# Folding a normalisation's mean into the weights of the first product of a ViT block

## The chip, the cores and the metric

One Trainium2 chip, one core of it. The metric is device time in microseconds of one execution, median over runs. All inputs lie in HBM before the kernel starts and the output is written back to HBM.

## The reference, cut to what matters

64 images of 3x96x96 are cut into 6x6 patches of 16x16x3 = 768 pixels. With `layernorm(x) = (x - mean) / sqrt(var + 1e-5)`:

```python
x = layernorm(x) * ln1_g + ln1_b             # over 768 pixels
x = x @ W + bias                             # 768 -> 256
x = layernorm(x) * ln2_g + ln2_b + pe        # over 256
h = concat(cls_token + cls_pos, x)           # 37 tokens an image
h = h + attention(layernorm(h))              # 16 heads of 16, rotary positions
h = h + ffn(layernorm(h))                    # 256 -> 1024 -> 256, ternary weights, 8-bit tokens
```

## The kernel before, in words

The 2368 tokens (class tokens included, as rows of zeros in x) lie in 19 tiles of 128 rows, `t` = 0 to 18, the last with 64 rows. The program has three stages: the patch stage (from pixels to rotated q and k and to values), attention over 32 pairs of images, and the feed-forward stage. The change is in the patch stage.

Each engine runs a list of instructions in the order in which it is written; semaphores (`S[...]`) tie the lists together. On each engine the patch stage is a loop over steps `s`, and `patch_step(s)` works on several tiles at once: the pixels of tile s or s + 1, the product's result of tile s - 2, the second normalisation of tile s - 3, and q, k and v of tile s - 9 and later (LAG is 9). So q, k and v begin at step 9; TensorE runs `early_step(s)` before that and `patch_step(s)` from then on. In one step:

- VectorE (DVE) takes statistics of the pixels (`pixel_stats`, L661, `pixel_mean`, L668, `pixel_var`, L674), statistics of the product's result (`y_stats`, L680, `y_mean`, L685, `y_var`, L690), centres and scales that result by ln2_g (`y_centre`, L695), makes h (`h_first`, L703) and takes its statistics (L709, L715, L720). From step 10 on it also rotates q and k (L775, L783).
- GpSimd (POOL) turns each variance into 1/sqrt (`inverse_root`, L1158), makes -mean/sd (`shift`, L1171), adds the two halves of the rotation (L1165) and writes the one-hot rows `hot` (L1187).
- ScalarE (ACT) normalises the pixels of a tile (`pixels_normal`, L979), copies the transposed pixels out of PSUM (`pixels_out`, L986), and does the same two things for h (L992, L999).
- TensorE (PE) turns the normalised pixels (six transposes, `turn_pixels`, L390), multiplies them by W (six f32 matmuls of 128x256, `patch_product`, L400), adds an offset row with a bf16 matmul on one-hot rows (`product_offset`, L383), puts the position rows into PSUM (`position_rows`, L383 too), turns h (`turn_h`, L430), and makes q, k and v (L443, L421). A f32 matmul stands as two in the profile.

Before the loop DVE multiplies W by ln1_g (L739, six instructions), TensorE makes the row ln1_b @ W (`patch_offset`, L369), and DVE and ACT split the offset and position rows into three bf16 parts that add up to f32 (L728, L1044, L1046). The SP queue loads the pixels and weights: x(0), the two halves of W, x(1), x(2), then the rest, where x(4) to x(7) each wait for a tile that ACT has normalised (`x_norm`). Five small loads go out on ACT's queue.

## Time and profile before

| | us |
|---|---|
| median of 3 runs | 355.41 (354.68 to 358.23) |
| the profiled execution, its own time | 358.58 |
| its span in the profile | 356.8 |
| PE busy | 310.9 (87%) |
| DVE busy | 247.1 (69%) |
| ACT busy | 214.6 (60%) |
| POOL busy | 136.8 (38%) |

A share of busy time is a mean over three stages with different limits, so the stages are read apart. In the span the patch stage reaches to about 175 us, attention to about 262 us, and the feed-forward stage to the end. The granted clock is TensorE's, as a share of its full speed.

### The profile page before, as it was taken

What the parts mean: (1) busy time and instruction counts of PE and PEld (TensorE: products, weight loads), DVE (VectorE), ACT (ScalarE), POOL (GpSimd) and SP (SyncE); (2) the same over time, 40 slices, a digit from 0 to 9 for tenths busy, and PEclk for the clock granted to TensorE, in tenths of its full rate; (3) what the DMA queues carried; (4) which work ended last, traced back from release to release, by engine and by line L of the source; (5) the groups of instructions that cost most, each with busy time, mean ns of one, the idle gap of its engine ahead of it and who ended that gap; (6) DMA issues with size and microseconds to landing.
All of it is one profiled execution on the core that took longest, in us unless ns stands there. A gap on an engine that the chain in (4) does not pass through costs nothing.

```text
span 356.8 us, 9434 instructions
## 1 busy us (share of the span) xinstructions
PE 310.9 (87%) x3582; PEld 235.8 (66%) x3590; DVE 247.1 (69%) x647; ACT 214.6 (60%) x385; POOL 136.8 (38%) x262
## 2 busy tenths in 40 slices
PE   7385767999999999799799999999976899999884
PEld 6274656777777765465488778778754677776553
DVE  2616647677566736245558787788758999999982
ACT  2224445447576453344556665665635999999992
POOL 1215453556545524444392000000035566555630
PEclk9878999999999999899989999999999999999998
DMA  7952991000000000001311121221100001000011
GB/s 230 264 187 88 376 322 33 3 17 33 16 16 32 17 18 17 31 31 49 72 38 40 42 50 39 45 45 40 25 3 1 2 24 38 29 31 29 30 46 51
DMA packets 19291, 22.30 MB, mean 63 GB/s; under 512 B 2304, under 2 KB 15888, under 8 KB 19248
## 3 DMA queue, kind: packets, MB, share of 16 engines
q1 hardware_dynamic: 18544, 20.89, 19.5%
q10 hardware_dynamic: 704, 0.82, 0.9%
q8 instruction: 29, 0.48, 0.6%
q14 instruction: 14, 0.11, 0.1%
HBM read 16.68 MB, written 5.02 MB: 61 GB/s over the span
## 4 chain that ended last, share of the span: by engine, by line
PE 62%; DVE 19%; ACT 8%; issue 5%; DMA 3%; POOL 2%; SPq 0%; DVEq 0%; ACTq 0%
PE ps L400 14%; PE ps L443 10%; PE ps L524 9%; PE ps L547 7%; DVE sc L900 7%; PE ps L421 4%; DVE ximg L921 4%; PE ps L514 4%; PE ps L390 3%; DMA ximg<-in_x 3%; PE ps L532 3%; ACT ximg L1124 3%; PE ps L383 2%; PE ps L451 2%; ACT ximg L1119 2%
## 5 line engine op out<-in xcount | busy, mean ns | idle before, releaser
L1158 POOL TENSOR_TENSOR rs<-rs,nhalf 128x1 f32<-128x1 f32 (+1 forms) x76 | 41.7, 556 | 181.4 <-DVE rs L894 100.5
L400 PE MATMUL ps<-w_in,xT 128*128 128x256 f32 (+1 forms) x228 | 56.6, 401 | 5.8 <-ACT xT L986 5.8
L400 PEld LDWEIGHTS ps<-w_in,xT 128*128 128x128 f32 (+1 forms) x228 | 43.9, 200 | 12.9 <-ACT xT L986 6.3
L1076 ACT ACTIVATE ximg<-ps 128x296 f32<-128x296 f32 x64 | 26.6, 418 | 31.4 <-PE ps L524 30.8
L443 PE MATMUL ps<-w_qk,hnT 128*128 128x512 f32 (+1 forms) x76 | 37.3, 615 | 2.3 <-DVE h L703 2.3
L775 DVE TENSOR_TENSOR qa<-ps,tab 128x512 f32<-128x512 f32 (+1 forms) x19 | 13.1, 691 | 36.9 <-PE ps L383 36.9
L838 DVE TENSOR_REDUCE ximg<-ps 128x16 f32<-128x592 f32 x32 | 24.7, 773 | 16.5 <-PE ps L514 16.4
L524 PE MATMUL ps<-tab,ximg 128*128 128x128 f32 x256 | 35.7, 283 | 0.0
L1165 POOL TENSOR_TENSOR qa<-qa,qb 128x512 f32<-128x512 f32 (+1 forms) x19 | 24.1, 1267 | 15.6 <-DVE qb L783 15.6
L524 PEld LDWEIGHTS ps<-tab,ximg 128*128 128x128 f32 x256 | 28.1, 143 | 1.3
L986 ACT ACTIVATE xT<-ps 128x768 f32<-128x768 f32 (+1 forms) x19 | 15.0, 791 | 22.4 <-PE ps L390 18.6
L979 ACT ACTIVATE xn<-ximg,nmr,rs 128x768 f32<-128x768 f32 (+1 forms) x19 | 19.4, 1020 | 14.4 <-POOL nmr L1171 13.6
L547 PE MATMUL ps<-ximg 128*37 128x34 f32 x1024 | 25.7, 203 | 2.2 <-issue 1.7
L547 PEld LDWEIGHTS ps<-ximg 128*37 128x37 f32 x1024 | 22.3, 117 | 7.0 <-issue 2.7
L390 PE MATMUL ps<-tab,xn 128*128 128x128 f32 (+1 forms) x114 | 15.9, 277 | 11.4 <-ACT xn L979 11.4
L842 DVE TENSOR_TENSOR ximg<-ps,ximg 128x592 f32<-128x592 f32 x32 | 24.8, 776 | 1.1
L1124 ACT ACTIVATE ximg<-ximg,magic,sc 128x1024 f32<-128x1024 f32 (+1 forms) x19 | 23.6, 1241 | 2.4 <-DVE sc L912 1.8
L921 DVE SCALAR_TENSOR_TENSOR ximg<-ps,sc,wide 128x1024 f32<-128x1024 f32 (+1 forms) x19 | 24.4, 1282 | 0.7 <-PE ps L606 0.7
L615 PE MATMUL ps<-tab,ximg 128*128 128x128 f32 (+1 forms) x152 | 20.0, 275 | 5.2 <-ACT ximg L1124 5.2
L900 DVE TENSOR_REDUCE sc<-ximg 128x1 f32<-128x1024 f32 (+1 forms) x19 | 23.0, 1209 | 2.1 <-ACT ximg L1119 1.8
L606 PE MATMUL ps<-w1t,ximg 128*128 128x512 bf16 (+1 forms) x68 | 18.1, 381 | 7.2 <-ACT ximg L1113 6.8
L999 ACT ACTIVATE hnT<-ps 128x256 f32<-128x256 f32 (+1 forms) x19 | 7.1, 373 | 26.8 <-PE ps L430 26.8
(107 smaller groups left out, 673.8 us busy)
## 6 DMA issues: line engine op xcount, KB each, us to landing
ximg<-in_x SPq DMA_DIRECT2D x18, 384.0 KB, 8.0
ximg<-vsc SPq DMA_DIRECT2D x64, 51.0 KB, 2.0
vsc<-vt SPq DMA_DIRECT2D x18, 136.0 KB, 1.7
out<-ximg SPq DMA_DIRECT2D x18, 128.0 KB, 1.7
ximg<-in_W SPq DMA_DIRECT2D x2, 1024.0 KB, 10.5
qkT<-in_W SPq DMA_DIRECT2D x2, 384.0 KB, 6.2
wide<-in_rows SPq DMA_DIRECT2D x1, 640.0 KB, 5.5
w_qk<-in_Wqk SPq DMA_DIRECT2D x1, 512.0 KB, 8.6
```

What stands on the lines that cost most here:

```text
L390: mm = pe.transpose(ps_xT[:, k, 0:n], xn[t % 2][0:n, 128 * k:128 * k + 128], ident[0:n, 0:n])
L400: pe.matmul(dst[0:n, :], xT[t % 2][:, k, 0:n], w_in[:, k, :], start=(k == 0), stop=False)
L443: pe.matmul(dst[0:n, :], hnT[t % HB][:, k, 0:n], w_qk[:, k, :], start=(k == 0), stop=False)
L524: mm = pe.transpose(ps[:, b, 128 * g:128 * g + 128], flat[:, at0:at0 + 128], ident)
L547: mm = pe.matmul(dst.rearrange("p (e c) -> p e c", e=2), pT[p % 2][:, g, i, :], rhs, start=True, stop=True)
L838: v.tensor_reduce(mx[u][:, :].rearrange("p (r h) -> p r h", r=4), ps_s, AX.X, ALU.max).then_inc(S["s_max"], 1)
L842: v.tensor_tensor(pr[u][:, :, 0:TOK].rearrange("p (r h) t -> p r h t", r=4), ps_s, mx[u][:, :].rearrange("p (r h) -> p r h", r=4).unsqueeze(3)
L900: v.tensor_reduce(sc[t % 8][0:n, c:c + 1], src[0:n, :], AX.X, ALU.max, apply_absolute_value=True).then_inc(S[f"{x}_amax"], 1)
L921: v.scalar_tensor_tensor(out=hd[t % 3][0:n, :], in0=ps_f[0:n, :], scalar=sc[t % 8][0:n, 3:4], in1=fb1[0:n, :], op0=ALU.mult, op1=ALU.add). ...
L1076: act.activation(pT[p % 2][:, g0:g0 + 4, :, :], ps_pT(b), ACT.Copy).then_inc(S[f"p_evac{b}"], 1)
L1124: act.activation(hd[t % 3][0:n, :], hd[t % 3][0:n, :], ACT.Identity, bias=magic[0:n, :], scale=sc[t % 8][0:n, 6:7]).then_inc(S["f_rnd"], 1)
L1158: pool.tensor_tensor(rs[u][0:n, i:i + 1], rs[u][0:n, i:i + 1], nhalf[0:n, :], ALU.pow).then_inc(S[done], 1)
```

## The change

The mean of a row of pixels is taken off through the weights. With W' = ln1_g * W and the mean over the 768 rows of W' taken off each of its columns, x @ W' no longer depends on the row's mean; the row's 1/sd is multiplied in behind the product, together with the offset row ln1_b @ W + bias.

- TensorE makes the column means before the loop (`weight_means`, six f32 matmuls with `g1s` = ln1_g / 768 as stationary operand), and DVE takes them off as it scales W (`w_in`, six instructions that read the mean row from PSUM, each with a semaphore increment of its own).
- ACT's `pixels_normal` is gone, and POOL's `shift` for pixels with it. TensorE turns the raw pixels as soon as they are loaded.
- DVE's new `y_scale` multiplies the product by 1/sd and adds `yoff`, from PSUM into the SBUF tile `ymid`; `y_stats` and `y_centre` read `ymid` instead of PSUM. It frees the product's PSUM bank, which `y_centre` did before.
- The offset's matmul on one-hot rows behind each product is gone. A class token's row is zeroed by POOL's new `leave_class`, which multiplies 1/sd of the second normalisation by a column of 0 and 1.
- DVE takes the pixel statistics of tile s - 1 in step s, where it took those of tile s + 1.
- The early steps of TensorE run the product of s - 1 ahead of the transposes of s; `patch_step` keeps its order but for the offset.
- On the SP queue the halves of W go out ahead of x(0), and no load of x waits for `x_norm`. The small offset and table loads grow by 64 KB and 10 KB.

```diff
+        g1s = sb("g1s", [128, KP])
+        yoff = sb("yoff", [128, D])
...
-            load_x(0)
             sp.dma_start(w_raw[:, 0:3, :], w_rows[:, 0:3, :]).then_inc(S["ld_w0"], 16)
             sp.dma_start(w_raw[:, 3:6, :], w_rows[:, 3:6, :]).then_inc(S["ld_w1"], 16)
+            load_x(0)
             load_x(1)
+            sp.wait_ge(S["ld_offs"], 16)
             load_x(2)
-            sp.wait_ge(S["ld_offs"], 16)
             load_x(3)
+            sp.dma_start(w_o[:], a["Wo"].rearrange("(k p) n -> p k n", p=128)).then_inc(S["ld_o"], 16)
             sp.dma_start(offs[0:112, 4 * D:7 * D], spread_row(a["offsets"][4 * D:7 * D], 3 * D, 112)).then_inc(S["ld_rows"], 16)
-            sp.dma_start(w_o[:], a["Wo"].rearrange("(k p) n -> p k n", p=128)).then_inc(S["ld_o"], 16)
-            sp.wait_ge(S["x_norm"], 1)
             load_x(4)
+            load_x(5)
             sp.dma_start(w_qk[:], a["Wqk"].rearrange("(k p) n -> p k n", p=128)).then_inc(S["ld_qk"], 16)
-            sp.wait_ge(S["x_norm"], 2)
-            load_x(5)
+            load_x(6)
             sp.dma_start(w_v[:], a["Wv"].rearrange("(k p) n -> p k n", p=128)).then_inc(S["ld_v"], 16)
-            sp.wait_ge(S["x_norm"], 3)
-            load_x(6)
+            load_x(7)
             sp.dma_start(tab[:, FTAB:NTAB], a["table"][:, FTAB:NTAB]).then_inc(S["ld_rot"], 16)
-            sp.wait_ge(S["x_norm"], 4)
-            load_x(7)
+            load_x(8)
             sp.dma_start(wide[:, D:2 * D + F], spread_row(a["rows"][D:2 * D + F], D + F)).then_inc(S["ld_wide"], 16)
-            for t in range(8, NT + 1):
+            for t in range(9, NT + 1):
...
+            def weight_means():
+
+                pe.wait_ge(S["g1_done"], 1)
+                for k in range(KP):
+                    if k % 3 == 0:
+                        pe.wait_ge(S[f"ld_w{k // 3}"], 16)
+                    mm = pe.matmul(ps_mean, bass.AP(g1s, k, [[KP, 128], [0, 128]]), w_raw[:, k, :],
+                                   start=(k == 0), stop=(k == KP - 1))
+                mm.then_inc(S["mrow"], 1)
+
             def patch_offset():
-                pe.wait_ge(S["ld_w0"], 16)
-                pe.wait_ge(S["ld_byp"], 16)
                 for k in range(KP):
-                    if k == 3:
-                        pe.wait_ge(S["ld_w1"], 16)
-                    mm = pe.matmul(ps[0:K3, 6, 0:D], bass.AP(byp, k, [[2 * KP + 2, 128], [0, K3]]), w_raw[:, k, :],
+                    mm = pe.matmul(ps_off, bass.AP(byp, k, [[2 * KP + 2, 128], [0, 128]]), w_raw[:, k, :],
                                    start=(k == 0), stop=(k == KP - 1))
                 mm.then_inc(S["crow"], 1)
...
             def turn_pixels(t):
-                pe.wait_ge(S["x_norm"], t + 1)
+                pe.wait_ge(ld_x[t], 16)
+                if t == 0:
+                    pe.wait_ge(S["ld_tab"], 16)
                 war(pe, "x_evac", t, 1)
                 n = rows(t)
                 for k in range(KP):
-                    mm = pe.transpose(ps_xT[:, k, 0:n], xn[t % 2][0:n, 128 * k:128 * k + 128], ident[0:n, 0:n])
+                    mm = pe.transpose(ps_xT[:, k, 0:n], ximg[0:n, t, 128 * k:128 * k + 128], ident[0:n, 0:n])
                 mm.then_inc(S["x_turned"], 1)
 
             def patch_product(t):
                 pe.wait_ge(S["x_evac"], t + 1)
-                war(pe, "y_mid", t)
-                if t == 0:
-                    pe.wait_ge(S["wg_done"], 2)
+                war(pe, "y_scaled", t)
+                if t == 16:
+                    pe.wait_ge(S["w_rc"], 1)
                 n, dst = rows(t), ps_y(t % 2)
                 for k in range(KP):
-                    pe.matmul(dst[0:n, :], xT[t % 2][:, k, 0:n], w_in[:, k, :], start=(k == 0), stop=False)
-                if t >= 2:
-                    product_offset(t)
-
-            def product_offset(t):
-
-                if t >= 2:
-                    pe.wait_ge(S["hot_done"], min(t, 16))
-                add_rows(ps_y(t % 2)[0:rows(t), :], t, C_ROWS).then_inc(S["y_ready"], 1)
+                    if t == 0:
+                        pe.wait_ge(S["wg_done"], k + 1)
+                    mm = pe.matmul(dst[0:n, :], xT[t % 2][:, k, 0:n], w_in[:, k, :], start=(k == 0),
+                                   stop=(k == KP - 1))
+                mm.then_inc(S["y_ready"], 1)
 
             def position_rows(t):
+                if t == 0:
+                    pe.wait_ge(S["b_done"], 1)
+                pe.wait_ge(S["hot_done"], max(1, min(t, 16)))
                 war(pe, "h_ready", t, 1)
                 add_rows(ps_pos[0:rows(t), :], t, PE_ROWS, only=True).then_inc(S["pos_ready"], 1)
...
             def early_step(s):
+                patch_product(s - 1)
                 turn_pixels(s)
-                patch_product(s - 1)
                 if s == 5:
                     out_offset()
-                position_rows(s - 2)
-                turn_h(s - 3)
+                if live(s - 2, NT + 1):
+                    position_rows(s - 2)
+                if live(s - 3, NT + 1):
+                    turn_h(s - 3)
...
+            weight_means()
+            turn_pixels(0)
             patch_offset()
-            pe.wait_ge(S["ld_tab"], 16)
-            turn_pixels(0)
-            patch_product(0)
-            turn_pixels(1)
-            patch_product(1)
-            turn_pixels(2)
-            pe.wait_ge(S["hot_done"], 1)
-            pe.wait_ge(S["b_done"], 1)
-            product_offset(0)
-            product_offset(1)
-            position_rows(0)
-            for s in range(3, LAG):
+            for s in range(1, LAG):
...
+            def y_scale(t):
+                v.wait_ge(S["y_ready"], t + 1)
+                v.wait_ge(S["x_rstd"], t + 1)
+                if t == 0:
+                    v.wait_ge(S["y_off"], 1)
+                n = rows(t)
+                v.scalar_tensor_tensor(out=ymid[t % 2][0:n, :], in0=ps_y(t % 2)[0:n, :], scalar=rs[t % 2][0:n, 0:1],
+                                       in1=yoff[0:n, :], op0=ALU.mult, op1=ALU.add).then_inc(S["y_scaled"], 1)
+
             def y_stats(t):
-                v.wait_ge(S["y_ready"], t + 1)
-                n = rows(t)
-                v.bn_stats(st[t % 2][0:n, 2, :], ps_y(t % 2)[0:n, :]).then_inc(S["y_stat"], 1)
+                v.wait_ge(S["y_scaled"], t + 1)
+                n = rows(t)
+                v.bn_stats(st[t % 2][0:n, 2, :], ymid[t % 2][0:n, :]).then_inc(S["y_stat"], 1)
...
-                v.scalar_tensor_tensor(out=ymid[t % 2][0:n, :], in0=ps_y(t % 2)[0:n, :], scalar=mv[t % 2][0:n, 1, 0:1],
+                v.scalar_tensor_tensor(out=ymid[t % 2][0:n, :], in0=ymid[t % 2][0:n, :], scalar=mv[t % 2][0:n, 1, 0:1],
...
+            v.wait_ge(S["ld_byp"], 16)
+            v.tensor_scalar(g1s[:, :], g1, 1.0 / PD, None, ALU.mult).then_inc(S["g1_done"], 1)
             pixel_stats(0)
             pixel_mean(0)
             pixel_var(0)
-            v.wait_ge(S["ld_byp"], 16)
-            for half in range(2):
-                v.wait_ge(S[f"ld_w{half}"], 16)
-                for k in range(3 * half, 3 * half + 3):
-                    ins = v.tensor_scalar(w_in[:, k, :], w_raw[:, k, :], g1[:, k:k + 1], None, ALU.mult)
-                ins.then_inc(S["wg_done"], 1)
+            v.wait_ge(S["mrow"], 1)
+            for k in range(KP):
+                v.scalar_tensor_tensor(out=w_in[:, k, :], in0=w_raw[:, k, :], scalar=g1[:, k:k + 1], in1=ps_mean,
+                                       op0=ALU.mult, op1=ALU.subtract).then_inc(S["wg_done"], 1)
             pixel_stats(1)
             pixel_mean(1)
             pixel_var(1)
+            v.wait_ge(S["ld_offs"], 16)
+            v.wait_ge(S["crow"], 1)
+            v.tensor_tensor(yoff[:, :], ps_off, bfix, ALU.add).then_inc(S["y_off"], 1)
             v.wait_ge(S["ld_tab"], 16)
-            v.wait_ge(S["ld_offs"], 16)
             v.tensor_tensor(cls0, cls0, cls1, ALU.add).then_inc(S["bmix"], 1)
             v.wait_ge(S["ld_pe"], 16)
...
+            y_scale(0)
+            y_stats(0)
             v.wait_ge(S["b_hi"], 1)
             leave_out(bres[0:K3, py], bhi[0:K3, py], 0, brow[0:K3, :]).then_inc(S["b_res"], 1)
+            y_mean(0)
+            y_var(0)
...
-                if live(s - 2, NT + 1):
-                    y_stats(s - 2)
+                if live(s - 2, NT + 1) and s > 2:
+                    y_scale(s - 2)
                 if s == 16:
                     weight_scales()
-                if live(s + 1, NT + 1):
-                    pixel_stats(s + 1)
-                if live(s - 2, NT + 1):
+                if live(s - 1, NT + 1) and s > 2:
+                    pixel_stats(s - 1)
+                if live(s - 2, NT + 1) and s > 2:
+                    y_stats(s - 2)
+                if live(s - 1, NT + 1) and s > 2:
+                    pixel_mean(s - 1)
+                if live(s - 2, NT + 1) and s > 2:
                     y_mean(s - 2)
-                if live(s + 1, NT + 1):
-                    pixel_mean(s + 1)
-                if live(s - 2, NT + 1):
                     y_var(s - 2)
-                if live(s + 1, NT + 1):
-                    pixel_var(s + 1)
+                if live(s - 1, NT + 1) and s > 2:
+                    pixel_var(s - 1)
...
-            def pixels_normal(t):
-                act.wait_ge(ld_x[t], 16)
-                act.wait_ge(S["x_nmr"], t + 1)
-                war(act, "x_turned", t)
-                n = rows(t)
-                act.activation(xn[t % 2][0:n, :], ximg[0:n, t, :], ACT.Identity, bias=nmr[t % 2][0:n, 0:1],
-                               scale=rs[t % 2][0:n, 0:1]).then_inc(S["x_norm"], 1)
...
+            def leave_class(t):
+
+                pool.wait_ge(S["y_root"], t + 1)
+                n = rows(t)
+                pool.tensor_tensor(rs[t % 2][0:n, 1:2], rs[t % 2][0:n, 1:2], tab[0:n, tile_o + t:tile_o + t + 1],
+                                   ALU.mult).then_inc(S["y_rstd"], 1)
...
-                    inverse_root(1, s - 2, s % 2, "y_var", "y_rstd")
-                if live(s + 1, NT + 1):
-                    inverse_root(0, s + 1, (s + 1) % 2, "x_var", "x_rstd")
-                    shift(0, 0, s + 1, "x_rstd", "x_nmr")
+                    inverse_root(1, s - 2, s % 2, "y_var", "y_root")
+                    leave_class(s - 2)
+                if live(s - 1, NT + 1) and s > 2:
+                    inverse_root(0, s - 1, (s - 1) % 2, "x_var", "x_rstd")
```

The start of TensorE's list before (`onesf` is the warm-up's operand, `tab` holds the identity, `xn` the normalised pixels, `xT` the turned ones, `hot` and `pos_rows` the one-hot and offset rows):

```order
L486 MATMUL ps<-onesf 128x128 x13
L369 MATMUL ps<-qkT,byp 111x256 x6
L390 MATMUL ps<-tab,xn 128x128 x6
L400 MATMUL ps<-w_in,xT 128x256 x6
L390 MATMUL ps<-tab,xn 128x128 x6
L400 MATMUL ps<-w_in,xT 128x256 x6
L390 MATMUL ps<-tab,xn 128x128 x6
L383 MATMUL ps<-pos_rows,hot 128x256 x3
```

And now, up to the first position rows (`ximg` holds raw pixels, W lies in `qkT` at this time):

```order
L499 MATMUL ps<-onesf 128x128 x13
L373 MATMUL ps<-qkT,g1s 128x256 x6
L402 MATMUL ps<-tab,ximg 128x128 x6
L379 MATMUL ps<-qkT,byp 128x256 x6
L414 MATMUL ps<-w_in,xT 128x256 x6
L402 MATMUL ps<-tab,ximg 128x128 x6
L414 MATMUL ps<-w_in,xT 128x256 x6
L402 MATMUL ps<-tab,ximg 128x128 x6
L393 MATMUL ps<-pos_rows,hot 128x256
```

The means of W come first, the transposes read the raw pixels, and the first two offset matmuls are gone.

DVE's list in an early step before, from the statistics of one product to the h made of it:

```order
L680 BN_STATS st<-ps 128x6
L661 BN_STATS st<-ximg 128x6 x2
L685 BN_AGGR mv<-st 128x2
L668 BN_AGGR mv<-st 128x2
L690 TENSOR_SCALAR rs<-mv 128x1
L674 TENSOR_SCALAR rs<-mv 128x1
L695 SCALAR_TENSOR_TENSOR ymid<-ps,mv,wide 128x256
L703 SCALAR_TENSOR_TENSOR h<-ymid,rs,ps 128x256
```

And now:

```order
L685 SCALAR_TENSOR_TENSOR ymid<-ps,rs,yoff 128x256
L665 BN_STATS st<-ximg 128x6 x2
L691 BN_STATS st<-ymid 128x6
L671 BN_AGGR mv<-st 128x2
L696 BN_AGGR mv<-st 128x2
L701 TENSOR_SCALAR rs<-mv 128x1
L676 TENSOR_SCALAR rs<-mv 128x1
L706 SCALAR_TENSOR_TENSOR ymid<-ymid,mv,wide 128x256
L714 SCALAR_TENSOR_TENSOR h<-ymid,rs,ps 128x256
```

One instruction more (L685), the statistics of the result behind those of the pixels, and L706 with both of its tensors in SBUF.

## Rows read from the trace of the kernel before

**Rows 1.** Stretch, length, busy us of PE, PEld, DVE, ACT, POOL; granted clock, DMA, GB/s

```profile
10.00:20.00 10.00, 5.01 (x19) 3.96 (x20) 6.97 (x18) 3.76 (x5) 3.75 (x6) 0.77 0.97 287
40.00:50.00 10.00, 6.31 (x35) 4.79 (x33) 6.43 (x25) 4.33 (x7) 5.51 (x15) 1.00 1.04 342
100.00:120.00 20.00, 20.00 (x103) 15.20 (x102) 12.74 (x43) 12.29 (x25) 10.66 (x20) 1.00 0.06 22
```

**Rows 2.** Waits from 0 to 66 us: total us, times, longest

```profile
DVE h L703 <- PE ps L383: 13.5, 4, 4.5
```

**Rows 3.** Timeline (start, us, engine, line, [idle before]): the start, all engines

```profile
3.89 1.02 DVE L661 BATCH_NORM_STATS2 st<-ximg 128x6 f32<-128x384 f32 x2 [2.88 <-DMA ximg<-in_x]
...
10.06 0.88 DVE L739 TENSOR_SCALAR w_in<-qkT,byp 128x256 f32<-128x256 f32 x3 [3.85 <-DMA qkT<-in_W]
...
17.20 5.33 PE L400 MATMUL ps<-w_in,xT 128*128 128x256 f32 x12 [4.92 <-ACT xT L986]
...
23.21 0.81 ACT L986 ACTIVATE xT<-ps 128x768 f32<-128x768 f32 x1 [3.19 <-PE ps L390]
24.07 2.46 PEld L400 LDWEIGHTS ps<-w_in,xT 128*128 128x128 f32 x12 [1.14 <-ACT xT L986]
...
30.12 0.48 DVE L703 SCALAR_TENSOR_TENSOR h<-ymid,rs,ps 128x256 f32<-128x256 f32 x1
```

**Rows 4.** Timeline: one unhindered turn of DVE's loop, with POOL beside it

```profile
57.61 1.00 DVE L661 BATCH_NORM_STATS2 st<-ximg 128x6 f32<-128x384 f32 x2
...
58.53 0.17 DVE L685 BATCH_NORM_AGGREGATE mv<-st 128x2 f32<-128x6 f32 x1
...
58.78 0.11 DVE L690 TENSOR_SCALAR rs<-mv 128x1 f32<-128x1 f32 x1
...
58.97 0.47 DVE L695 SCALAR_TENSOR_TENSOR ymid<-ps,mv,wide 128x256 f32<-128x256 f32 x1
58.97 1.06 POOL L1158 TENSOR_TENSOR rs<-rs,nhalf 128x1 f32<-128x1 f32 x2 [0.60 <-DVE rs L690]
...
59.55 0.48 DVE L703 SCALAR_TENSOR_TENSOR h<-ymid,rs,ps 128x256 f32<-128x256 f32 x1
...
60.07 0.43 DVE L709 BATCH_NORM_STATS2 st<-h 128x6 f32<-128x256 f32 x1
...
60.82 0.42 DVE L680 BATCH_NORM_STATS2 st<-ps 128x6 f32<-128x256 f32 x1
```

**Rows 5.** Timeline: PE at the first instruction of step 9, and DVE behind it

```profile
65.92 0.28 PE L383 MATMUL ps<-pos_rows,hot 111*128 111x256 bf16 x1 [0.46 <-DVE h L703]
...
66.25 1.00 DVE L728 SCALAR_TENSOR_TENSOR pos_rows<-qkT,tab 111x768 bf16<-111x768 bf16 x1
```

**Rows 6.** Timeline: POOL's shift beside a DVE instruction with two SBUF inputs

```profile
14.71 0.48 DVE L751 SCALAR_TENSOR_TENSOR qkT<-qkT,tab 111x256 f32<-111x256 f32 x1
14.79 0.53 POOL L1171 TENSOR_SCALAR nmr<-mv,rs 128x1 f32<-128x1 f32 x1
```

**Rows 7.** The line of that shift: duration ns min/median/max over the kernel

```profile
L1171 POOL TENSOR_SCALAR nmr<-mv,rs x38: 257/265/550, 6.3 to 149.7; 128x1 f32<-128x1 f32 x36, 64x1 f32<-64x1 f32 x2
```

**Rows 8.** Timeline: PE through a step of the later patch stage

```profile
99.77 0.27 PE L383 MATMUL ps<-pos_rows,hot 111*128 111x256 bf16 x1
...
100.32 2.76 PE L400 MATMUL ps<-w_in,xT 128*128 128x256 f32 x12
102.92 0.28 PE L383 MATMUL ps<-pos_rows,hot 111*128 111x256 bf16 x1
103.03 0.82 PE L390 MATMUL ps<-tab,xn 128*128 128x128 f32 x6
...
106.71 0.27 PE L383 MATMUL ps<-pos_rows,hot 111*128 111x256 bf16 x1
```

**Rows 9.** Timeline: the stall at the end of the products

```profile
143.94 0.47 DVE L703 SCALAR_TENSOR_TENSOR h<-ymid,rs,ps 64x256 f32<-64x256 f32 x1 [1.04 <-POOL rs L1158]
...
144.56 3.22 PE L443 MATMUL ps<-w_qk,hnT 128*128 128x512 f32 x4 [2.26 <-DVE h L703]
```

More of the change, by code:

```diff
@@ L73, in shape_constants @@
             pe[r] = np.concatenate([np.sin(ax), np.cos(ax), np.sin(ay), np.cos(ay)])
-    return np.concatenate([np.eye(128), vmask, pmask, taken, patch, ~patch, hot, pe,
+    return np.concatenate([np.eye(128), vmask, pmask, taken, patch, ~patch, hot, by_tile, pe,
                            cos.reshape(128, -1), sin.reshape(128, -1)], 1).astype(np.float32)
-FTAB = 128 + NH + 2 + 2 + 2 + TOK + D
+FTAB = 128 + NH + 2 + 2 + 2 + TOK + NT + 1 + D
 NTAB = FTAB + 2 * (NT + 1) * HD
@@ L212, in two @@
             return [sb(f"{name}{u}", shape, dt) for u in range(2)]
-        xn = two("xn", [128, PD])
         xT = two("xT", [128, KP, 128])
@@ L729, in leave_out @@
                                               op0=ALU.mult, op1=ALU.add)
-            qo, py = slice(2 * D, 5 * D), slice(0, 2 * D)
+            qo, py = slice(D, 4 * D), slice(0, D)
+            v.wait_ge(S["ld_byp"], 16)
+            v.tensor_scalar(g1s[:, :], g1, 1.0 / PD, None, ALU.mult).then_inc(S["g1_done"], 1)
             pixel_stats(0)
@@ L1037, in patch_step @@
                     pixels_out(s)
-            pixels_normal(0)
-            pixels_normal(1)
             pixels_out(0)
-            qo, py = slice(2 * D, 5 * D), slice(0, 2 * D)
-            act.wait_ge(S["bmix"], 5)
+            pixels_out(1)
+            qo, py = slice(D, 4 * D), slice(0, D)
+            act.wait_ge(S["bmix"], 3)
             act.activation(bhi[0:K3, py], brow[0:K3, :], ACT.Copy).then_inc(S["b_hi"], 1)
@@ L1046, in _ @@
             act.activation(bmid[0:K3, py], bres[0:K3, py], ACT.Copy).then_inc(S["b_mid"], 1)
-            pixels_normal(2)
-            pixels_out(1)
             pixels_out(2)
@@ L1205, in _ @@
                 patch_step(s)
-            pool.wait_ge(S["x_norm"], NT)
+            pool.wait_ge(S["y_scaled"], NT)
+            for u in range(2):
+                ins = pool.memset(pr[u][:, :, TOK:64], 0.0)
+            ins.then_inc(S["p_zero"], 1)
             for u in range(4):
@@ L1210, in _ @@
                 patch_step(NT + 3 + u)
-            for u in range(2):
-                ins = pool.memset(pr[u][:, :, TOK:64], 0.0)
-            ins.then_inc(S["p_zero"], 1)
             for s in range(NT + 7, NT + LAG + 2):
```

45 lines of the change are left out of this document (18 added, 27 removed).

## The prediction

> **What bounds the kernel now.** I read the stretches of the span first, then the waits of the first 66 us, then the timeline of three places: the start, the early steps, and one late step. Late in the patch stage TensorE is never idle: 20.00 us busy of 20, at a granted clock of 1.00 [rows 1]. A step takes 106.71 - 99.77 = 6.94 us there [rows 8], all of it TensorE's. [...] In the first 66 us DVE waits 13.5 us, in four waits, for the position rows that TensorE writes late [rows 2], because its transposes wait for ACT's normalised pixels, and these for 1/sd from POOL. At the start TensorE is idle 4.92 us ahead of its first product and runs that at the lower clock, 5.33 us for twelve records against 2.76 later [rows 3, 8]. The first h is made at 30.12 us and step 9 begins at 65.92 [rows 3, 5], so the six turns of the early loop between them took 5.9 us each, where an unhindered turn of DVE takes 3.5 (60.82 - 57.61, and 0.33 for the first statistics [rows 4]). What is saved ahead of 65.92 moves all that follows; work taken off ACT in the late steps moves nothing.
>
> **The start, walked with the new lists.** The third transfer of SP's queue (the second half of W) let DVE go at 10.06, and the first (x(0)) had landed at 3.89 [rows 3]. Now x(0) is the third, with 74 KB more on the other queue, which at the 287 GB/s of the stretch from 10 us on [rows 1] is 0.3 us: x(0) at 10.4, both halves of W long before. The column means are a product's six matmuls, 102.92 - 100.32 = 2.6 us [rows 8], from the end of the warm-up at 6.0, so they are done at 8.6, under the wait for x(0). The statistics of x(0) come ahead of the scaling of W on DVE and take 1.45 us, to 11.85. The six scalings now read PSUM and the mean row, and I cost them like h's STT at 59.55, 0.50 each by start to start [rows 4], where plain ones took 0.29 [rows 3]: W' complete at 14.85, 3.0 us against 1.8. TensorE meanwhile turns x(0), 0.65 us (0.82 less the overlap [rows 8]), makes the offset row to 13.7, and runs the first product, which follows the slices of W', to 16.3. The second one waits for its transposes (16.9), ACT's copy and 0.86 us from the copy's start to the product's [rows 3], and ends at 20.6; the third transposes at 21.25, then the position rows of tile 0. DVE does the statistics of x(1) to 16.3, four row instructions of 0.48 to 18.2, `y_scale` and `y_stats` to 19.2, and the three-way split with ACT, at half the width of before, in some 1.6 to 20.8, so both sides meet and the first h is made at **21.6**, 8.5 us earlier. Lower bound: DVE alone, 21.3. [...]
>
> **The early steps.** Two loops could set them. TensorE's: transposes 0.82 to their end, then ACT's copy to the product 0.86, then the product 2.60 [rows 3, 8], together 4.3 us; the product now stands ahead of the next transposes, so ACT's copy is no longer hidden there. DVE's, from `y_scale` round to the next: `y_scale` 0.45 (between the 0.35 of an offset-free stats start and the 0.52 of h's), pixel statistics 58.53 - 57.61 = 0.92, `y_stats` 0.42, the first aggregate 0.15, the second aggregate to POOL's root 58.97 - 58.53 = 0.44, root to h (below), h to its statistics 0.52, and those to the next step 60.82 - 60.07 = 0.75 [rows 4]. Root to h was 59.55 - 58.97 = 0.58. It gets `leave_class` in between, which no row shows. Its ends are POOL's shift, 0.27 [rows 7], and its root, the same kind of instruction on the same size with a power, 0.53 of a pair in 1.06 [rows 4]; I take 0.27, because it multiplies as the shift does, plus 0.10 to issue. And `y_centre` now reads two SBUF tensors, starting when POOL's root starts (both at 58.97 [rows 4]). Such a pair stands at 14.7: a shift beside a DVE instruction with two SBUF inputs took 0.53 and ended 0.13 behind it, where the median is 0.265 and only a few rows reach 0.55 [rows 6, 7]. So POOL's reads waited. The root then ends about 0.33 later (DVE's 0.47, plus the root's own 0.41 behind its reads, less the usual 0.55). Root to h: 0.58 + 0.37 + 0.33 = 1.28. The loop is 0.45 + 0.92 + 0.42 + 0.15 + 0.44 + 1.28 + 0.52 + 0.75 = **4.93 us**, so DVE with POOL sets the pace, not TensorE. Bounds of the turn: 4.6 without the collision, 5.2 with `leave_class` at 0.53.
>
> [...]
>
> Six turns are 29.6 us; two inserted instructions (the add at step 5, 0.5, and the 768-wide split at step 6, 1.0 as its like [rows 5]) were there before too. From 21.6 this gives h of tile 6 at 52.7 and step 9 at 53.2 instead of 65.92: **-12.7 us**. The loads keep up: up to x(8) they are 6.8 MB, 24 us at the 287 GB/s of the second slice [rows 1], and x(8) is turned at about 48.
>
> **The late steps.** The offset matmul goes, 103.03 - 102.92 = 0.11 us of TensorE [rows 8], in the eleven tiles from 8 to 18: **-1.2 us**. DVE was busy 12.74 of 20 us [rows 1], 4.4 us a step; what the early turn gains, 4.93 - 3.54 = 1.4, makes it 5.8, still inside 6.83, so TensorE stays full. ACT's 1.03 us less a tile is worth nothing here. At the end of the products TensorE stood 2.26 us for the last h, which waited for POOL's root, and this costs it the clock too [rows 9]; `leave_class` adds 0.4 to that wait: **+0.4 us**. POOL clears the attention's buffers in another order, behind which nobody waits by 161 us. Attention and feed-forward do not change.
>
> **Sum.** -12.7 - 1.2 + 0.4 = -13.5 us. On the profiled execution, 358.58, that is 345.1; it stands 3.2 us above the median of the three runs, 355.41, and the change is at places all runs share, so I forecast the median **342.0 us**.
>
> **Rivals.**
> (a) The pace of the early steps does not fall. If some other hand-over (`h_normal` ahead of `pixels_out` on ACT, TensorE in order behind `turn_h`) keeps a turn at 5.9, only the start is won: 355.4 - 8.5 - 1.2 + 0.4 = 346.3. For it: the old loop also had 3.5 us of DVE work and took 5.9. Against: the waits that made it so hang on the normalised pixels, which are gone. 0.16.
> (b) No collision and short hand-overs, a turn of 4.6: 2.0 us better, 340.0; with a little less at the start, 338.5. 0.17.
> (c) TensorE loses its clock. In the early steps it will work 3.6 of 4.9 us. [...] For it: after gaps of 4.9 and 2.26 us the clock was low [rows 3, 9]. Against: from 40 to 50 us TensorE was busy 6.3 of 10 us and had 1.00 [rows 1]. Slower 0.03, about even 0.03.
> [...]
> (d) DVE's late step outgrows 6.83. [...] It is the lesser brother of (a) and I give it 0.06.
> The forecast's own case has 0.55.
>
> **Range and chances.** The forecast's case spans 339.5 to 345 by the bounds of the turn (6 x 0.3 either way) and 1 us of landing time. (b) reaches to 338, (a) and (d) to 346.5, and the runs of one kernel here differ by 3.5 us. 337.5 to 347.5 leaves out (c) and the tails, under 2 in 10. A measurement of this kernel can tell about 1%, 3.6 us, from no change: faster 0.94, same 0.03, slower 0.03.
>
> **What would show it.** TensorE's first product near 13.7 us at the full clock; the first h at 21 to 22; h of the early tiles 4.9 us apart, with POOL's root beside `y_centre` at 0.8 to 0.9 instead of 0.55; the first q and k product near 57 instead of 69; later steps 6.83 us apart and TensorE without idle time; the stall at the last tile 2.7 us long. It is wrong if DVE waits for TensorE in the early steps, if the granted clock of 10 to 50 us stays below 0.9, or if the late steps grow.

## The result, and the profile after

The changed kernel takes 341.55 us (median of 4 runs, 340.69 to 343.08), the kernel before 355.22 in the same series (354.68 to 358.23): a ratio of 0.9605, 95% interval 0.9549 to 0.966. The forecast was 342.0, with 337.5 to 347.5 as its range. The profiled execution took 343.08 against 358.58, its span 341.3 against 356.8; the text below accounts for these 15.5 us.

Busy times of the whole span, after:

```profile
PE 310.8 (91%) x3583; PEld 235.1 (69%) x3583; DVE 254.7 (75%) x666; ACT 197.1 (58%) x366; POOL 139.6 (41%) x262
```

ACT lost 17.5 us of work (197.1 against 214.6), DVE gained 7.6, TensorE is as busy as before. So what was saved is TensorE's waiting. The stretches, with the columns of [rows 1]:

```profile
10.00:20.00 10.00, 9.10 (x48) 7.83 (x47) 8.04 (x22) 2.34 (x4) 4.26 (x7) 1.00 0.96 324
...
40.00:50.00 10.00, 7.36 (x40) 5.67 (x38) 8.33 (x28) 3.87 (x7) 5.79 (x13) 1.00 0.62 211
50.00:60.00 10.00, 9.64 (x37) 7.21 (x38) 7.61 (x23) 2.50 (x5) 4.93 (x11) 0.83 0.01 2
...
100.00:120.00 20.00, 20.00 (x100) 14.89 (x99) 14.43 (x47) 8.45 (x20) 10.17 (x18) 1.00 0.06 22
```

From 10 to 20 us TensorE went from 5.01 busy at a clock of 0.77 to 9.10 at 1.00. The one bad row is new: from 50 to 60 us the clock is 0.83. The kernel before had low rows early, too, 0.77, 0.89 and 0.83 from 10 to 40 us. In the first of its six turns:

```profile
32.12 1.26 PE L390 MATMUL ps<-tab,xn 128*128 128x128 f32 x6 [4.21 <-ACT xn L979]
33.17 4.10 PE L400 MATMUL ps<-w_in,xT 128*128 128x256 f32 x12
```

These two took 1.8 us more than the 0.82 and 2.75 of the full clock, and the first product (5.33) took 2.6 more. So I estimate that some 4.4 us of the gain up to step 9 are clock that the kernel before had lost behind its waits; no run separates them from the shorter chain. DVE's waits for h in the first 53 us (step 9 begins at 50), as in [rows 2], which go to 66 us:

```profile
DVE h L714 <- POOL rs L1169: 3.6, 5, 0.7
DVE h L714 <- PE ps L393: 2.7, 2, 1.6
```

DVE's 13.5 us of waiting for the position rows has shrunk to 2.7, and five waits of 0.7 us for `leave_class` (L1169) on POOL have come in. One of the two waits for position rows is the first h, the other the third turn, where TensorE has the added work of step 5:

```profile
35.00 0.48 DVE L714 SCALAR_TENSOR_TENSOR h<-ymid,rs,ps 128x256 f32<-128x256 f32 x1 [1.07 <-PE ps L393]
```

The start, against [rows 3]:

```profile
6.74 3.01 PE L373 MATMUL ps<-qkT,g1s 128*128 128x256 f32 x12
8.66 1.02 DVE L665 BATCH_NORM_STATS2 st<-ximg 128x6 f32<-128x384 f32 x2 [4.75 <-DMA ximg<-in_x]
...
10.03 2.43 DVE L750 SCALAR_TENSOR_TENSOR w_in<-qkT,byp,ps 128x256 f32<-128x256 f32 x6
10.24 2.76 PE L379 MATMUL ps<-qkT,byp 128*128 128x256 f32 x12
...
12.83 2.75 PE L414 MATMUL ps<-w_in,xT 128*128 128x256 f32 x12
...
20.90 0.48 DVE L714 SCALAR_TENSOR_TENSOR h<-ymid,rs,ps 128x256 f32<-128x256 f32 x1 [1.62 <-PE ps L393]
```

Means, transposes, offset row and first product now follow one another on TensorE with little between them, and the product runs at the full clock. One turn of the early loop, from one h to the next, DVE and POOL:

```profile
25.48 0.48 DVE L714 SCALAR_TENSOR_TENSOR h<-ymid,rs,ps 128x256 f32<-128x256 f32 x1 [0.71 <-POOL rs L1169]
...
26.75 0.48 DVE L685 SCALAR_TENSOR_TENSOR ymid<-ps,rs,yoff 128x256 f32<-128x256 f32 x1
...
27.15 1.01 DVE L665 BATCH_NORM_STATS2 st<-ximg 128x6 f32<-128x384 f32 x2
...
28.08 0.41 DVE L691 BATCH_NORM_STATS2 st<-ymid 128x6 f32<-128x256 f32 x1
...
28.87 0.48 DVE L706 SCALAR_TENSOR_TENSOR ymid<-ymid,mv,wide 128x256 f32<-128x256 f32 x1
28.98 0.78 POOL L1156 TENSOR_TENSOR rs<-rs,nhalf 128x1 f32<-128x1 f32 x1 [1.13 <-DVE rs L701]
...
29.83 0.19 POOL L1169 TENSOR_TENSOR rs<-rs,tab 128x1 f32<-128x1 f32 x1
29.97 0.55 POOL L1156 TENSOR_TENSOR rs<-rs,nhalf 128x1 f32<-128x1 f32 x1
30.06 0.48 DVE L714 SCALAR_TENSOR_TENSOR h<-ymid,rs,ps 128x256 f32<-128x256 f32 x1 [0.71 <-POOL rs L1169]
```

30.06 - 25.48 = 4.58 us. The root beside `y_centre` took 0.78, the root of the pixels that follows it 0.55. Last, TensorE at step 9, at step 10 and at the last tile, against [rows 5] and [rows 9]:

```profile
50.36 0.27 PE L393 MATMUL ps<-pos_rows,hot 111*128 111x256 bf16 x1 [1.71 <-DVE h L714]
50.62 4.49 PE L414 MATMUL ps<-w_in,xT 128*128 128x256 f32 x12
...
58.65 0.28 PE L393 MATMUL ps<-pos_rows,hot 111*128 111x256 bf16 x1
...
130.05 3.65 PE L454 MATMUL ps<-w_qk,hnT 128*128 128x512 f32 x4 [2.70 <-DVE h L714]
```

Ahead of step 9 stands a wait of 1.71 us. The step itself, from 50.36 to 58.65, takes 8.29 us, and its product 4.49 where 2.75 is usual. Before, step 10 began here:

```profile
72.48 0.27 PE L383 MATMUL ps<-pos_rows,hot 111*128 111x256 bf16 x1
```

Step 9 took 72.48 - 65.92 = 6.56 us.

Where the 15.5 us came from, from landmarks of both traces:

| stretch | before | after | difference | forecast |
|---|---|---|---|---|
| up to the first h | 30.12 | 20.90 | -9.2 | -8.5 |
| to the start of step 9 | 35.80 | 29.46 | -6.3 | -4.2 |
| step 9 | 6.56 | 8.29 | +1.7 | -0.1 |
| to the stall at the last tile | 69.82 | 68.70 | -1.1 | -1.1 |
| that stall | 2.26 | 2.70 | +0.4 | +0.4 |
| behind it | 212.2 | 211.2 | -1.0 | 0 |

The terms add up to -15.5. The last row is none of the change's: the final 36.8 us of the trace before had a granted clock of 0.95, the same work after (35.8 us) had 1.00, and at the scores of the first attention group (166.05 and 151.54) the kernels are 14.5 apart. Ten of the twelve traces of the changed kernel and its variants also had a low clock (0.70 to 0.90) from 330 to 340 us. The medians differ by 13.7.

### The profile page after: what moved, and what is told of

Read it like the earlier page. It is cut to its first block, busy times and chain, and to the rows that moved or that the text cites. A ratio compares the mean times of both kernels' runs of the same rounds, so it can differ in the third digit from the quotient of the medians.

```text
span 341.3 us, 9410 instructions
## 1 busy us (share of the span) xinstructions
PE 310.8 (91%) x3583; PEld 235.1 (69%) x3583; DVE 254.7 (75%) x666; ACT 197.1 (58%) x366; POOL 139.6 (41%) x262
## 4 chain that ended last, share of the span: by engine, by line
PE 65%; DVE 20%; ACT 7%; issue 4%; POOL 2%; DVEq 0%
PE ps L414 13%; PE ps L454 10%; PE ps L528 9%; PE ps L551 7%; DVE sc L911 7%; PE ps L432 5%; PE ps L518 4%; DVE ximg L932 4%; PE ps L402 3%; PE ps L536 3%; ACT ximg L1122 3%; PE ps L462 2%; ACT ximg L1117 2%; PE ps L393 2%; PE ps L499 2%
## 5 line engine op out<-in xcount | busy, mean ns | idle before, releaser
L1156 POOL TENSOR_TENSOR rs<-rs,nhalf 128x1 f32<-128x1 f32 (+1 forms) x76 | 46.2, 607 | 164.4 <-DVE rs L905 100.8
L414 PE MATMUL ps<-w_in,xT 128*128 128x256 f32 (+1 forms) x228 | 54.8, 391 | 3.6 <-ACT xT L989 3.6
L414 PEld LDWEIGHTS ps<-w_in,xT 128*128 128x128 f32 (+1 forms) x228 | 42.2, 191 | 11.3 <-ACT xT L989 5.1
L528 PE MATMUL ps<-tab,ximg 128*128 128x128 f32 x256 | 35.8, 284 | 0.0
L610 PE MATMUL ps<-w1t,ximg 128*128 128x512 bf16 (+1 forms) x76 | 19.7, 382 | 5.7 <-ACT ximg L1111 5.6
L665 DVE BATCH_NORM_STATS2 st<-ximg 128x6 f32<-128x384 f32 (+1 forms) x38 | 19.2, 546 | 4.7 <-DMA ximg<-in_x 4.7
L1079 ACT ACTIVATE ximg<-ximg 128x592 f32<-128x592 f32 x32 | 22.6, 706 | 0.0
```

Source lines behind the costliest of these rows:

```text
L414: mm = pe.matmul(dst[0:n, :], xT[t % 2][:, k, 0:n], w_in[:, k, :], start=(k == 0), stop=(k == KP - 1))
L528: mm = pe.transpose(ps[:, b, 128 * g:128 * g + 128], flat[:, at0:at0 + 128], ident)
L1156: pool.tensor_tensor(rs[u][0:n, i:i + 1], rs[u][0:n, i:i + 1], nhalf[0:n, :], ALU.pow).then_inc(S[done], 1)
```

## The experiments

Each ratio below is against runs of the kernel before on the same chip; the runs were made in four groups, each on a chip of its own, so medians of different groups are compared by their ratios. Where and when the clock fell shows only in a trace, and each kernel has one. Five questions were open: what the load order is worth, what sets the early turn, whether ACT's relief matters, whether DVE has room late, and why step 9 is slow.

**The changed kernel again**, beside the next three:

> The changed kernel once more, as the reference of this group. 341.5 us, a ratio of 0.961 to the kernel before; first h near 20.9 us, step 9 of TensorE near 50.4 us, its product at the lower clock (4.5 us for twelve records against 2.76).

343.61 us, 0.9595 (0.9555 to 0.9636): the result stands. First h 20.72, step 9 at 50.18, its product 4.51 us long.

**Only the SP queue of the change** (order of the loads, and no load of x waiting for `x_norm`), in the kernel before:

```diff
-            load_x(0)
...
+            load_x(0)
...
-            sp.wait_ge(S["x_norm"], 1)
...
-            for t in range(8, NT + 1):
+            for t in range(9, NT + 1):
```

> The kernel before with only the SP queue of the change: W ahead of x(0), and no load of x waiting for a normalised tile. My theory: the gain comes from the shorter chain of hand-overs, not from the loads, so this is within 1 us of the kernel before (355). Rival: the loads carry the start, and with them alone the first h comes 5 us or more earlier and the time falls to 350 or below.

357.6 us, 1.0002 (0.9966 to 1.0038): nothing, as expected. Its first h is made at 29.21 instead of 30.12, and that is given back in the turns.

**x(0) first**, in the changed kernel:

```diff
+            load_x(0)
             sp.dma_start(w_raw[:, 0:3, :], w_rows[:, 0:3, :])
             sp.dma_start(w_raw[:, 3:6, :], w_rows[:, 3:6, :])
-            load_x(0)
```

> The changed kernel with x(0) ahead of the two halves of W on the SP queue. My theory: the start hangs on the third transfer of that queue, whichever it is. With W's second half third, the means of W end at about 11.4 instead of 9.6 us, W' is complete near 14.0 instead of 12.5, and the first h comes 1.2 to 1.6 us later; in time +1.2 to +1.6 us against the changed kernel. Rival: the order of the first three loads is indifferent, since both sides wait for both: 0.

345.88 us, 0.9676 (0.9627 to 0.9724). TensorE in the middle of the means:

```profile
10.01 1.56 PE L373 MATMUL ps<-qkT,g1s 128*128 128x256 f32 x6 [2.02 <-DMA qkT<-in_W]
```

The first h comes at 22.73, 2.0 us later than in the unchanged copy beside it, and the median is 2.3 later. That is more than the 1.2 to 1.6 expected. So the queue's new order is worth nothing by itself, and losing the one part of it that puts W ahead of x(0) costs 2 us once the means have to be read from W. Here the same wait of 1.71 us stood at step 9, and the product behind it took 2.83 us: the clock did not fall there. It fell at the last tile, whose product took 3.75.

**The scaled product stays in PSUM**, which takes one SBUF input from `y_centre` (POOL's root takes 0.78 us beside it):

```diff
-                v.scalar_tensor_tensor(out=ymid[t % 2][0:n, :], in0=ps_y(t % 2)[0:n, :], ...
+                v.scalar_tensor_tensor(out=ps_y(t % 2)[0:n, :], in0=ps_y(t % 2)[0:n, :], ...
```

The statistics and `y_centre` read `ps_y`, and TensorE's next product waits for `y_mid` instead of `y_scaled`.

> The changed kernel, with y_scale writing back to the product's PSUM bank; y_stats and y_centre read that, so y_centre has one SBUF input again. [...]

Expected were a root of 0.55 us, root to h in 0.85 instead of 1.08, a turn of 4.41 and 1 us in the time; if the root stayed at 0.78, nothing. Measured: 339.88 us, 0.9501 (0.9457 to 0.9545). The first two turns are 4.41 us, the last 4.35. `y_centre`, the root and h:

```profile
23.85 0.47 DVE L706 SCALAR_TENSOR_TENSOR ymid<-ps,mv,wide 128x256 f32<-128x256 f32 x1
23.96 0.55 POOL L1156 TENSOR_TENSOR rs<-rs,nhalf 128x1 f32<-128x1 f32 x1 [1.13 <-DVE rs L701]
...
24.87 0.48 DVE L714 SCALAR_TENSOR_TENSOR h<-ymid,rs,ps 128x256 f32<-128x256 f32 x1 [0.54 <-POOL rs L1169]
```

Same instructions, same moment, one operand in another memory: the root takes 0.55 instead of 0.78, `y_centre` 0.47 both times. The collision is real, costs POOL 0.23, and never held DVE's `y_centre`. The last turn shows it in full (4.58 - 0.23); in the first two TensorE's loop ends at 4.41, and with the added work of step 5 the third is 5.28, against 4.95 in `act_copy` (below) on the same chip. So the six turns together are 28.15 us, against 28.82 there: 0.7 us, where 1 us was expected. The median moved by 3.4 us (0.0094 of 357.8). What goes with the rest is the clock: in this trace it fell neither at step 9 nor at the last tile. That this is the effect of the edit is not shown.

```profile
49.23 0.27 PE L393 MATMUL ps<-pos_rows,hot 111*128 111x256 bf16 x1 [1.49 <-DVE h L714]
49.36 2.83 PE L414 MATMUL ps<-w_in,xT 128*128 128x256 f32 x12
...
126.91 1.95 PE L454 MATMUL ps<-w_qk,hnT 128*128 128x512 f32 x4 [2.52 <-DVE h L714]
```

**ACT gets its work back**: the raw pixels are copied by ACT before TensorE turns them, in the early steps too.

```diff
+                act.activation(xn[t % 2][0:n, :], ximg[0:n, t, :], ACT.Copy).then_inc(S["x_norm"], 1)
...
-                    mm = pe.transpose(ps_xT[:, k, 0:n], ximg[0:n, t, ...
+                    mm = pe.transpose(ps_xT[:, k, 0:n], xn[t % 2][0:n, ...
```

> The changed kernel with a copy of the raw pixels by ACT (1.03 us a tile) put back between load and transposes; statistics and 1/sd stay behind the product. My theory: the gain came from taking DVE's statistics and POOL's 1/sd out of the way to the transposes, not from the work that ACT is spared; so the early turns stay at 4.6 us, the late steps at 6.81 us, and the time rises by less than 1 us. Rival: the hop over ACT itself was the price; then the early turns go back towards 5.5 us or more and the time rises by 5 us.

343.6 us, 0.9594 (0.9554 to 0.9635): the same as without the copy. Turns are 4.58, late steps 6.81, and the product of step 9 took 2.83 behind its wait of 1.71. So ACT's time as such is free. That the early steps before were held by the dependence of ACT's output on POOL's 1/sd is then argued from the waits of the kernel before, here from 0 to 160 us (total, times, longest):

```profile
ACT xn L979 <- POOL nmr L1171: 13.6, 6, 7.7
PE ps L390 <- ACT xn L979: 11.4, 4, 4.2
```

The change also moved DVE's pixel statistics and TensorE's order; no run took these apart from it.

**One more DVE instruction a step**, in one kernel in steps 3 to 8, in another in steps 11 to 19:

```diff
+                if 3 <= s <= 8:
+                    v.bn_stats(spare[:, :], yoff[:, :])
```

> The changed kernel with one more DVE instruction (statistics of a 256 wide SBUF row, 0.42 us, result unused) behind y_scale in steps 3 to 8. My theory: DVE and POOL set the pace of the early turns, so each turn grows by 0.35 to 0.42 us, from 4.58 to 4.95 or 5.0, step 9 begins 2.3 us later and the time rises by 2.3 us. Rival: TensorE with ACT's copy sets the pace (4.41 us a turn), and the addition is hidden in part or whole, under 1 us.

> The changed kernel with the same added DVE instruction in steps 11 to 19 instead. My theory: TensorE is full there (6.81 us a step) and DVE has 1.1 us to spare, so the steps stay at 6.81 us and the time does not move (0 to 0.5 us, the half for step 19). Rival: DVE's longer step is already at the limit, and nine steps cost 3 to 4 us.

Early, DVE's h of the tiles:

```profile
25.33 0.48 DVE L715 SCALAR_TENSOR_TENSOR h<-ymid,rs,ps 128x256 f32<-128x256 f32 x1 [0.71 <-POOL rs L1172]
30.24 0.48 DVE L715 SCALAR_TENSOR_TENSOR h<-ymid,rs,ps 128x256 f32<-128x256 f32 x1 [0.71 <-POOL rs L1172]
35.14 0.48 DVE L715 SCALAR_TENSOR_TENSOR h<-ymid,rs,ps 128x256 f32<-128x256 f32 x1 [0.71 <-POOL rs L1172]
```

A turn is 4.90 us, 0.32 more, and the six turns take 30.40 us instead of 28.83. Five of the six were lengthened, by about 0.32 us each, so DVE with POOL sets the pace in them. The third was not (4.90 against 4.94): there TensorE, with the added work of step 5, set it before. Step 9 began 1.6 us later than in `act_copy` (51.46 against 49.88), where 2.3 was expected. The time itself is inconclusive: 342.45 us, 0.9568 (0.9512 to 0.9624), and the 1.6 us did not show in it. The runs go from 340.43 to 346.14. The trace is that of the longest run, whose product of step 9 took 5.42 us. Late, TensorE through two steps:

```profile
85.00 0.27 PE L394 MATMUL ps<-pos_rows,hot 111*128 111x256 bf16 x1
...
91.82 0.27 PE L394 MATMUL ps<-pos_rows,hot 111*128 111x256 bf16 x1
```

And a stretch of it, with the columns of [rows 1]:

```profile
100.00:120.00 20.00, 20.00 (x101) 14.79 (x99) 15.41 (x50) 8.44 (x21) 10.06 (x18) 1.00 0.07 22
```

Steps stay at 6.82, TensorE is never idle although DVE is busy 15.41 of 20 us, and the time is 344.28 us, 0.9609 (0.9558 to 0.966), that of the changed kernel. DVE has room there for this 0.4 us a step.

**The product of step 9 goes first**, ahead of the position rows that wait for DVE:

```diff
             def patch_step(s):
+                if s == 9:
+                    patch_product(s - 1)
+                    turn_pixels(s)
                 if live(s - 2, NT + 1):
                     position_rows(s - 2)
...
-                if live(s - 1, NT + 1):
+                if s > 9 and live(s - 1, NT + 1):
```

> The changed kernel, with TensorE in step 9 running the product of tile 8 and the transposes of tile 9 ahead of the position rows of tile 7, for which it waits 1.7 us today. My theory: that idle time (2.1 us from the end of the work before) and the lower clock behind it (4.49 against 2.76 us) are both lost to one wait, so both come back: step 10 begins near 55.6 instead of 58.65 us and the time falls by 3 us, to a ratio near 0.952. Rival: DVE sets the pace over step 10 too, and only the clock's 1.7 us or less comes back; or the clock falls at another place of the early steps and nothing is won.

340.69 us, 0.952 (0.9475 to 0.9566).

```profile
48.43 2.86 PE L414 MATMUL ps<-w_in,xT 128*128 128x256 f32 x12 [0.26 <-ACT xT L992]
...
55.25 0.27 PE L393 MATMUL ps<-pos_rows,hot 111*128 111x256 bf16 x1 [0.18 <-DVE h L717]
```

The product starts in what was the wait, at the full clock, and step 10 begins at 55.25 instead of 58.33. Of these 3.1 us, 1.65 are the shorter product (4.51 - 2.86), the rest is the wait that it fills. The kernel as a whole is 2.9 us under the copy beside it (343.61), as expected; the two intervals overlap by 0.001. The trace is that of its fastest run (338.99), and its clock was kept at the last tile too (1.96), which the edit does not touch.

**Filling both waits** of TensorE with matmuls on ones, whose result nobody reads, first too many (12 and 18, below), then as many as fit (7 and 11):

```diff
+                if s == 9:
+                    keep_busy(ps[:, 7, 0:128], 12)
...
+                if s == 20:
+                    pe.wait_ge(S["y_scaled"], 18)
+                    keep_busy(ps[:, 3, 0:128], 18)
```

> The changed kernel with matmuls of no use where TensorE waits longest: twelve f32 ones of 128x128 on ones ahead of the position rows of step 9, where it stands 1.7 us, and eighteen ahead of the q and k product of step 20, where it stands 2.7 us. They write PSUM that nobody reads, and fit into the waits. [...]

> The filled waits once more, at the right size. In the first attempt a f32 matmul of 128x128 took 0.22 us, not the 0.11 that I had counted, so 12 and 18 of them outlasted the waits by 0.6 and 1.3 us. Now 7 (1.6 us in a wait of 1.7) and 11 (2.4 us in one of 2.7). [...]

That the idle time is what lowers the clock was my supposition. With it I expected up to 3.5 us of the first (4.49 - 2.76 at step 9, 3.65 - 1.9 at the last tile) and 339.7 us, 0.950, of the second; if the clock fell all the same, no gain.

Too many: 341.47 us, 0.9556 (0.9507 to 0.9604); the fills lasted 2.84 and 4.18 us and overran the waits by some 0.6 and 1.3, with both products behind them at the full clock (2.75 and 1.88). This interval overlaps that of the changed kernel, so its gain is not clear. As many as fit: 340.85 us, 0.9518 (0.949 to 0.9545).

```profile
48.28 1.73 PE L482 MATMUL ps<-onesf 128*128 128x128 f32 x14
50.15 0.27 PE L393 MATMUL ps<-pos_rows,hot 111*128 111x256 bf16 x1
50.28 2.83 PE L414 MATMUL ps<-w_in,xT 128*128 128x256 f32 x12
...
125.15 2.62 PE L482 MATMUL ps<-onesf 128*128 128x128 f32 x22
128.02 1.96 PE L454 MATMUL ps<-w_qk,hnT 128*128 128x512 f32 x4 [0.25 <-DVE h L723]
```

Step 9 begins at 50.15, as in the changed kernel (50.18 and 50.36), so nothing came earlier; only the clock was kept. The ratio is 0.0077 under that of the changed kernel, 2.8 us, and the intervals just miss each other (0.9545 and 0.9555). The two traces alone would prove little, since unfilled waits kept the clock in some traces too. But the mean granted clock of every run is on record: it is 0.995 in 7 of the 12 runs with filled waits, and 0.99 or less in all 20 runs of the changed kernel, its copy, `act_copy` and `dve_late`. Two products at the lower clock cost 1.7 us each where they occur (4.49 - 2.83 and 3.65 - 1.95), 3.4 us in an execution that has both.

**What they point to.** `leave_class` goes from POOL into `y_var` on DVE, the scaled product stays in PSUM, and step 9's product goes first; the second kernel also turns the next pixels ahead of the product in the early steps, since TensorE now sets the turn.

```diff
-                v.tensor_scalar(rs[t % 2][0:n, 1:2], mv[t % 2][0:n, 1, 1:2], EPS, None, ALU.add
+                v.tensor_scalar(rs[t % 2][0:n, 1:2], mv[t % 2][0:n, 1, 1:2], EPS, tab[0:n, tile_o + t:tile_o + t + 1],
+                                ALU.add, ALU.mult).then_inc(S["y_var"], 1)
...
-                    leave_class(s - 2)
```

and, in the second kernel only:

```diff
+                if s > 2:
+                    turn_pixels(s)
                 patch_product(s - 1)
-                turn_pixels(s)
+                if s <= 2:
+                    turn_pixels(s)
```

> Three edits on the changed kernel: y_scale writes back to PSUM; the zeroing of class tokens sits in DVE's y_var as a second operand (variance times 1e30 in those rows, whose root is then about zero), so POOL's leave_class is gone; and in step 9 the product of tile 8 and the transposes of tile 9 go ahead of the position rows. My theory: DVE's early turn falls under TensorE's 4.41 us, which sets the pace (1 us won over six turns), step 9 gives its 3 us, and the last wait gets 0.5 us shorter: 4.5 us in all, a ratio near 0.947. Rival: the parts overlap, and it is no better than the step 9 edit alone (0.952).

> The combination above, and TensorE's early steps from 3 on in the order of the kernel before: transposes of s ahead of the product of s - 1, which hides ACT's copy out of PSUM behind that product. My theory: TensorE's loop falls from 4.41 to about 3.6 us, DVE's own of 4.0 us sets the pace (4.58, less 0.23 for the root and 0.34 for leave_class), and six turns give another 2 to 2.4 us: 6.5 us in all, a ratio near 0.942. Rival: ACT, which copies the pixels out only behind h_normal, holds the turn at 4.4 us or more, and this is no faster than the combination.

The first: 340.41 us, 0.9517 (0.9465 to 0.9569), no better than step 9's product alone (0.952), as its rival said. Its first two turns are 4.41 like those of the scaled product in PSUM, and DVE waits 0.48 us for TensorE in them; all six take 27.54 us. TensorE begins the last tile's q and k product 1.2 us earlier than with step 9's product alone (125.55 against 126.73), but in this trace the clock fell there (3.61 us against 1.96). The mean clock is 0.983 or less in 4 of its 6 runs and in none of the other's, so the clock may be what hides the gain; no run shows it by itself. The second: 337.7 us (335.87 to 338.96), 0.9451 (0.9401 to 0.9501), the lowest median of all and faster than both kernels; its interval still overlaps that of the scaled product in PSUM (0.9501).

```profile
28.85 0.48 DVE L720 SCALAR_TENSOR_TENSOR h<-ymid,rs,ps 128x256 f32<-128x256 f32 x1 [0.21 <-POOL rs L1162]
33.10 0.48 DVE L720 SCALAR_TENSOR_TENSOR h<-ymid,rs,ps 128x256 f32<-128x256 f32 x1 [0.32 <-POOL rs L1162]
...
123.88 1.95 PE L454 MATMUL ps<-w_qk,hnT 128*128 128x512 f32 x4 [2.26 <-DVE h L720]
```

Turns are 4.14 to 4.43, but for the one of 4.95 with the 768-wide split, all six 26.26 us, and the stall at the last tile is back at 2.26 us, what it was in [rows 9].

## Why the prediction was right, step by step

**The start: the gain was nearly right (-8.5 against -9.2), though three of its terms were wrong.** x(0) landed at 8.66, not 10.4, and W' was scaled in 0.40 us a slice, not 0.50. Little of that came through: the means ended at 9.75 instead of 8.6 (the warm-up ran to 6.9, and the six matmuls took 3.01), and W' was ready ahead of TensorE. So the means and the offset row on TensorE set the start. It began the offset row at 10.24 and the first product at 12.83, 0.9 before the forecast. From there TensorE's chain went as walked, and the first h came 0.7 us before its forecast. The walk had assumed that x(0), as the third load, sets the start; `x0_first` and `loads_only` show that the order matters with the fold and not without.

**The early turn: right engine, 0.35 us too long.** Root to h took 1.08, not 1.28: the collision added 0.23 instead of 0.33, and `leave_class` 0.27 with its issue instead of 0.37. The working let root and `y_centre` start together; the root started 0.11 behind it, and with that the working itself gives the measured end (28.87 + 0.48 + 0.41 = 29.76). The rest is `y_scale` (0.40, not 0.45) and the statistics and aggregates behind it (0.33 and 0.11, not 0.42 and 0.15). Six turns make 2.1 of the 2.9 us by which step 9 began before its forecast; the start makes 0.7. The measured turn lies at the bound that the working gave for "no collision" (4.6), yet the collision is there: rival (b)'s time was nearly right and its mechanism is refuted by 0.78 against 0.55. In all six turns the root started 0.10 or 0.11 us behind `y_centre`, which took 0.47 to 0.48. So no run here shows what the two do in the other order, and the traces show when the root ended, not what held it.

One sign that the prediction named against itself did occur once: in the third turn DVE waited 1.07 us for TensorE. It had counted the added work of step 5 as 0.5 us of DVE's; TensorE's part of that work cost 0.36 in the third turn (4.94 - 4.58), and DVE's 0.19 in the fourth.

**Rival (a)** is refuted by the 4.58. `act_copy` rules out ACT's time as the reason of the old 5.9; that it was the dependence on 1/sd is argued from the waits above. Some 1.8 us of the old six turns were TensorE's lower clock in the first of them.

**Late steps and stall: as forecast.** 6.81 to 6.83 a step, TensorE without idle time, and 2.70 us at the last tile. `dve_late` refutes rival (d) with 15.41 of 20 us of DVE. The forecast had DVE's late step at 5.8 us; 14.43 of 20 us is 4.9, because it had carried over the whole growth of the early turn, waits included. The longer step of (d), up to 346.5 in the range, stands in no run.

**Step 9: not foreseen.** The forecast let the gain of step 9's start pass undiminished to step 10. But the early turn is DVE's, TensorE finishes ahead of it, and step 9 begins with the one instruction that needs DVE's last h. So TensorE stood 1.71 us, in this trace it lost its clock, and the step took 8.29 instead of 6.56 - 0.11. The wait itself lies ahead of the step and was in the forecast's turns; the loss of the clock was not. That takes back 1.8 of the 2.9 us that the start and the turns had given beyond the forecast. Two errors of opposite sign kept the total near it, and that is luck. It is a small relative of rival (c): the clock was lost in one step rather than in the whole stretch, where it stayed at 1.00 up to 50 us. At the start, where the forecast had TensorE waiting from 8.6 to 10.4 us, that wait did not come: x(0) landed under the means, TensorE was busy 9.10 of the 10 us from 10 to 20, and the granted clock was 1.00 from 10 to 50 us. No run here has a low clock over the whole stretch, so what (c) would have cost is not shown.

**The sum** -13.5 against -13.7 in the medians is thus closer than the terms deserve; in the profiled execution it was -15.5, 1.0 of it a clock that had been low in the trace before. The errors of the terms are 0.7 us (start), 2.1 (turns) and 1.8 (step 9).

What stays open: why the clock fell behind the same idle time in some traces (the changed kernel, `after_ref`, `dve_late`) and not in others (`x0_first`, `act_copy`), and with that how the gain of the change divides between the shorter chain and the kept clock, and how the medians divide between the shorter turn and the kept clock in `scale_in_psum`. And `dve_early`'s 1.6 us are seen in the trace but not in the time.

## What to carry to other kernels

Where engines hand one tile round, look for the dependence and not for the work: an instruction that hangs on a late scalar (here the normalised pixels on 1/sd) can be replaced by more work on an engine that has room. Then walk the border between the fast loop and the next phase, with the engine that has become early: the instruction that it meets first must not be the one that needs the late engine, or its idle time can cost the clock on top (here 1.7 us, in three of the five traces with the same wait of 1.71). And keep one operand of a DVE instruction in PSUM where it runs beside a POOL instruction that others wait for; here POOL's root took 0.55 us so, against 0.78, and that was worth 0.23 us a turn.
